# A two-layer spectral convolution kernel: the layout of small row loads in the last pass and of the spectrum tile in the second

## The reference, cut to what matters

```python
def _L0_conv_ref(x, weight_re, weight_im, bias):      # spectral convolution, 4 heads of 16 channels
    x_freq = jnp.fft.rfft2(x, axes=(-2, -1))
    core = jnp.einsum('bhixy,hioxy->bhoxy', xf[:, :, :, :32, :17], weight)   # 32 x 17 modes only
    out_freq = zeros.at[:, :, :, :32, :17].set(core)
    return jnp.fft.irfft2(out_freq, s=(H, W), axes=(-2, -1)) + bias

def _L1_conv_ref(x, gamma, beta):                     # a norm in hyperbolic space, over channels
    mu = m / sqrt(max(m[0]**2 - sum(m[1:]**2), EPS))  # m: mean of every channel over all pixels
    alpha = max(xf[:, 0] * mu[0] - xf[:, 1:] @ mu[1:], 1 + EPS)
    d = arccosh(alpha); var = mean(d * d)             # over all pixels of all images
    ...                                               # per pixel factors, then per channel
    return concatenate([sqrt(1 + sum(s * s)), s])

x = x + _L0_conv_ref(_gn(x), ...)
x = x + _L1_conv_ref(_gn(x), ...)
```

## Time and profile before

| what | us |
|---|---|
| median of three runs | 3980.3 |
| the three runs | 4032.01, 3980.3, 3980.14 |
| the profiled execution, its own time | 4024.94 |
| its span, first to last instruction | 4023.4 |
| first pass, roughly | 0 to 1120 |
| second pass | 1152 to 2060 |
| third pass | 2082 to 4023 |

### The profile page before, as it was taken

The page is one execution under the profiler, slowest core; times in us unless marked ns, Lnnn a source line. Parts: engine busy times, 40 slices in busy tenths (PEclk is TensorE's granted clock), DMA queues, the critical chain, the costliest instruction groups (busy, mean ns, idle before and its releaser), DMA issues. The chain is left out here.

```text
span 4023.4 us, 77883 instructions
## 1 busy us (share of the span) xinstructions
PE 3002.5 (75%) x26018; PEld 1495.1 (37%) x26018; DVE 2748.0 (68%) x2969; ACT 2141.8 (53%) x2940; POOL 1513.6 (38%) x876
## 2 busy tenths in 40 slices
PE   6988898989446767677715877877777778877776
PEld 3555555555211222222203434344333344443332
DVE  1888888888865355555444767677777677777766
ACT  6777676767200011111014767677776677776665
POOL 0110101010111111111113766666666666666666
PEclk9988888988668888888857999999999999999999
DMA  9878777677269999999915989899999899999898
GB/s 373 287 256 282 260 265 274 244 285 253 76 259 354 325 341 376 362 361 374 334 53 183 337 313 329 313 325 321 313 315 320 306 330 334 329 334 311 311 314 288
DMA packets 280512, 1199.08 MB, mean 298 GB/s; under 512 B 35145, under 2 KB 37038, under 8 KB 197934
## 3 DMA queue, kind: packets, MB, share of 16 engines
q1 hardware_dynamic: 266126, 1152.07, 79.9%
q0 software_dynamic: 14112, 43.37, 3.4%
HBM read 883.53 MB, written 311.73 MB: 297 GB/s over the span
## 5 line engine op out<-in xcount | busy, mean ns | idle before, releaser
L1323 POOL TENSOR_TENSOR c_ot<-c_ot,c_pp 128x1024 f32<-128x1024 f32 x512 | 1211.8, 2368 | 727.0 <-DVE c_ot L1272 651.8
L1262 DVE SCALAR_TENSOR_TENSOR c_xt<-c_xt,keep_k,c_p_u 128x1024 f32<-128x1024 f32 x512 | 654.0, 1277 | 332.5 <-DMA c_xt<-in_x 170.8
L1118 PE MATMUL c_p_u<-c_mv,c_zc 64*128 64x256 f32 x4096 | 612.3, 420 | 225.1 <-DVE c_xt L1262 163.1
L1272 DVE SCALAR_TENSOR_TENSOR c_ot<-c_p_f,keep_k,c_xt 128x1024 f32<-128x1024 f32 x512 | 657.3, 1284 | 177.0 <-DMA out<-c_ot 134.4
L1198 ACT ACTIVATE c_pp<-c_p_p,c_cols 128x1024 f32<-128x1024 f32 x512 | 570.5, 1114 | 362.4 <-PE c_p_p L1132 359.0
L1205 ACT ACTIVATE c_sq<-c_xt,c_cols 128x1024 f32<-128x1024 f32 x512 | 584.2, 1141 | 139.5 <-DVE c_xt L1262 138.8
L1118 PEld LDWEIGHTS c_p_u<-c_mv,c_zc 64*128 64x128 f32 x4096 | 371.4, 195 | 532.9 <-DVE c_xt L1262 321.3
L327 ACT ACTIVATE a_junk<-a_xt 128x1024 bf16<-128x1024 f32 x512 | 537.2, 1053 | 28.8 <-DMA a_xt<-in_x 21.5
L246 PE MATMUL a_p_rows<-a_xt,a_dft_h 128*64 128x512 f32 x2048 | 517.5, 652 | 33.6 <-DMA a_bias_t<-in_bias 19.5
L1132 PE MATMUL c_p_f<-c_rt,c_lwc 64*128 64x512 bf16 x1024 | 328.0, 402 | 179.6 <-DVE c_ot L1272 161.3
L663 PE MATMUL b_p_al<-b_xt,b_awc 128*32 128x512 f32 x2048 | 312.4, 682 | 161.2 <-DMA b_xt<-in_x 116.3
(11 more groups left out here) (209 smaller groups left out, 3029.8 us busy)
## 6 DMA issues: line engine op xcount, KB each, us to landing
a_xt<-in_x SPq DMA_DIRECT2D x256, 1024.0 KB, 8.0
b_xt<-in_x SPq DMA_DIRECT2D x128, 2048.0 KB, 16.0
c_xt<-in_x SPq DMA_DIRECT2D x256, 1024.0 KB, 16.7
out<-c_ot SPq DMA_DIRECT2D x256, 1024.0 KB, 18.4
maps<-b_maps POOLq DMA_DIRECT2D x64, 192.0 KB, 5.7
dmap<-b_dmap POOLq DMA_DIRECT2D x16, 768.0 KB, 11.6
c_rt<-maps SPq DMA_DIRECT2D x512, 24.0 KB
c_dmap<-dmap SPq DMA_DIRECT2D x16, 768.0 KB, 17.2
```

The lines of the kernel that those rows point to most:

```text
L1118: last = nc.tensor.matmul(p_u[:, 512 * at + W * r:512 * at + W * r + W], zc[t // CH][64 * at:64 * at + 64, i], mv[t % NB][64 * at:64 * at ...
L1262: V.scalar_tensor_tensor(out=u, in0=u, scalar=kc, in1=p_u[:], op0=ALU.mult, op1=ALU.add).then_inc(u_done, 1)
L1272: V.scalar_tensor_tensor(out=ot[t % NB][:, at], in0=p_f[:], scalar=kinv, in1=xt[t % NB][:, at], op0=ALU.add, op1=ALU.mult).then_inc(f_done, 1)
L1323: P.tensor_tensor(o, o, pp[n][:], ALU.add).then_inc(o_done, 1)
```

## The change

There are three edits.

1. **Third pass, rows of `rt`.** The rows are no longer the first 12 partitions of each half. They stand at partitions 5, 15, ... 115 (twelve rows, the two halves together), 14, 30, ... 126 (eight rows) and 16, 48, 80, 112 (four rows); `misc` masks follow. One load brings the rows of both halves, so a tile has three loads of 12, 8 and 4 rows in place of six of 6, 4, 2, 6, 4 and 2. The bytes are the same. The spectrum tile `ys` and its transform `idft` use every second partition of 128 in place of the first 64, and channel 0 goes out in one store in place of four.
2. **Second pass, spectrum tile.** `spt` and `prod` have 128 partitions with 32 channels each in place of 64 partitions with 64 channels. The sums over channels come out as two partial sums, on partitions 0 to 63 and 64 to 127, which the matmul of `layer_rows` adds, since `idft_h` now holds the transform twice. The factors by channel are copied once to `ah` and `lh` in the new layout. The modes come in four loads in place of two.
3. The semaphore counts follow.

```diff
+MAP_ROWS = ((5, 10), (14, 16), (16, 32))
...
-    for at, first in ((12, 0), (18, 64)):
-        for part, (row, rows) in enumerate(((0, 6), (6, 4), (10, 2))):
-            for s in range(2):
-                m[first + row + s:first + row + rows:2, at + 2 * part + s] = 1.0
+    for a, at in enumerate((12, 18)):
+        for part, ((first, step), rows) in enumerate(zip(MAP_ROWS, (6, 4, 2))):
+            for i in range(rows):
+                m[first + step * (rows * a + i), at + 2 * part + i % 2] = 1.0
...
-        spt = sb("spt", [64, C, YS])
-        prod = sb("prod", [64, C, M2])
+        spt = sb("spt", [128, C // 2, YS])
+        prod = sb("prod", [128, C // 2, M2])
...
-                for k in range(2):
-                    pool.dma_start(spt[KX * k:KX * k + KX].rearrange("k (h i) m -> k h (i m)", h=HEADS),
-                                   spec[b, k].rearrange("(h k) n -> k h n", h=HEADS)).then_inc(sp_in, 16)
+                for h in range(HEADS):
+                    half, i = 64 * (h // 2), 16 * (h % 2)
+                    pool.dma_start(spt[half:half + 64, i:i + 16].rearrange("p i m -> p (i m)"),
+                                   spec[b, :, KX * h:KX * h + KX]).then_inc(sp_in, 16)
...
-                ch.step(V.tensor_tensor(prod[:], spt[:, :, 0:M2], over_m(arow[0:64, b]), ALU.mult))
+                ch.step(V.tensor_tensor(prod[:], spt[:, :, 0:M2], over_m(ah[:, b]), ALU.mult))
...
-                V.tensor_reduce(vm[0:64, 0], prod[:].rearrange("p c m -> p m c"), AX_X, ALU.add).then_inc(v_ready, 1)
+                V.tensor_reduce(vm[:, 0], prod[:].rearrange("p c m -> p m c"), AX_X, ALU.add).then_inc(v_ready, 1)
...
+            for half in range(2):
+                p, c = slice(64 * half, 64 * half + 64), slice(32 * half, 32 * half + 32)
+                ch.inc(V.tensor_copy(ah[p], arow[p, :, c]))
+                ch.inc(V.tensor_copy(lh[p], lrow[p, :, c]))
...
-    maps_v = io["maps"].rearrange("b m s (t n) -> b t (m s) n", n=TC)
+    maps_v = io["maps"].rearrange("b (a m) s (t n) -> b t a (m s) n", a=2, n=TC)
...
+                for (first, step), rows in zip(MAP_ROWS, (6, 4, 2)):
+                    sp.dma_start(r[first:first + step * (2 * rows - 1) + 1:step], maps_v[b, t, :, :rows]).then_inc(r_in[t % NB], 16)
                 for at in range(2):
-                    for row, rows in ((0, 6), (6, 4), (10, 2)):
-                        sp.dma_start(r[64 * at + row:64 * at + row + rows], maps_v[b, t, 6 * at:6 * at + rows]).then_inc(r_in[t % NB], 16)
...
-                    sp.dma_start(ys[KX * k:KX * k + KX, 32 * half:32 * half + 32].rearrange("k (h i) m -> k h (i m)", h=2),
+                    sp.dma_start(ys[64 * k:64 * k + 64:2, 32 * half:32 * half + 32].rearrange("k (h i) m -> k h (i m)", h=2),
...
-                for j in range(4):
-                    sp.dma_start(o0_v[b, 0, j], o0[32 * j:32 * j + 32]).then_inc(o0_out, 16)
+                sp.dma_start(o0_v[b, 0], o0[:]).then_inc(o0_out, 16)
```

More of the change, by code:

```diff
@@ L578, in stage_b @@
     uw_ready, uw_out, aw_ready, var_ready = sem("uw_ready"), sem("uw_out"), sem("aw_ready"), sem("var_ready")
-    NC_IN = 16 * 16
+    NC_IN = 16 * 17
     with ExitStack() as mem:
@@ L595, in stage_b @@
         arow, lrow = sb("arow", [128, B, C]), sb("lrow", [128, B, C])
+        ah, lh = sb("ah", [128, B, C // 2]), sb("lh", [128, B, C // 2])
         aw, awc = sb("aw", [128, B, 2, 2]), sb("awc", [128, 2, 47])
@@ L634, in _ @@
             sp.dma_start(btrow[:], row(io["beta"], C)).then_inc(c_in, 16)
-            sp.dma_start(idft_h[0:64], cst["idft_d"]).then_inc(c_in, 16)
+            for half in range(2):
+                sp.dma_start(idft_h[64 * half:64 * half + 64], cst["idft_d"]).then_inc(c_in, 16)
             sp.dma_start(idft_w[:], cst["idft_w"]).then_inc(c_in, 16)
@@ L814, in combine @@
             def combine(b):
-                dve.wait_ge(sp_in, b * 32 + 32)
-                over_m = lambda a: a.unsqueeze(2).to_broadcast((64, C, M2))
-                ch.step(V.tensor_tensor(prod[:], spt[:, :, 0:M2], over_m(arow[0:64, b]), ALU.mult))
+                dve.wait_ge(sp_in, b * 64 + 64)
+                over_m = lambda a: a.unsqueeze(2).to_broadcast((128, C // 2, M2))
+                ch.step(V.tensor_tensor(prod[:], spt[:, :, 0:M2], over_m(ah[:, b]), ALU.mult))
                 if not is_at(b, 0):
                     dve.wait_ge(z_mm, b)
-                V.tensor_reduce(vm[0:64, 0], prod[:].rearrange("p c m -> p m c"), AX_X, ALU.add).then_inc(v_ready, 1)
-                V.tensor_copy(vm[0:64, 1], spt[:, 0, 0:M2]).then_inc(v_ready, 1)
+                V.tensor_reduce(vm[:, 0], prod[:].rearrange("p c m -> p m c"), AX_X, ALU.add).then_inc(v_ready, 1)
+                V.tensor_copy(vm[0:64, 1], spt[0:64, 0, 0:M2]).then_inc(v_ready, 1)
                 dve.wait_ge(v_ready, b * 3 + 2)
-                ch.step(V.tensor_tensor(prod[:], spt[:, :, 0:M2], over_m(lrow[0:64, b]), ALU.mult))
-                V.tensor_reduce(vm[0:64, 2], prod[:].rearrange("p c m -> p m c"), AX_X, ALU.add).then_inc(v_ready, 1)
+                ch.step(V.tensor_tensor(prod[:], spt[:, :, 0:M2], over_m(lh[:, b]), ALU.mult))
+                V.tensor_reduce(vm[:, 2], prod[:].rearrange("p c m -> p m c"), AX_X, ALU.add).then_inc(v_ready, 1)
                 dve.wait_ge(v_ready, b * 3 + 3)
@@ L892, in _ @@
             ch.inc(V.memset(uw[:], 0.0))
[L893 to L894 removed]
+            V.memset(vm[:], 0.0).then_inc(setup, 1)
             dve.wait_ge(c_in, NC_IN)
@@ L1074, in entry @@
                             load_modes(b + 1, half)
-            sp.wait_ge(zeroed, 2 * NB + 2)
+            sp.wait_ge(zeroed, 2 * NB + 3)
             for half in range(2):
                 load_modes(0, half)
-            sp.dma_start(idft[0:64].rearrange("p a b c -> p (a b c)"), cst["idft_c"]).then_inc(c_in, 16)
+            sp.dma_start(idft[0:128:2].rearrange("p a b c -> p (a b c)"), cst["idft_c"]).then_inc(c_in, 16)
             sp.dma_start(misc[:], cst["misc"]).then_inc(c_in, 16)
@@ L1095, in _ @@
             store_channel_0(B - 1)
-            sp.wait_ge(o0_out, B * 64)
+            sp.wait_ge(o0_out, B * 16)
         @block.tensor
@@ L1164, in _ @@
             pe.wait_ge(c_in, 16 * (2 + 2 * NB))
-            pe.wait_ge(filled, 3)
+            pe.wait_ge(filled, 2)
             for part in range(8):
@@ L1239, in _ @@
             columns(0)
-            act.wait_ge(zeroed, 2 * NB + 2)
-            act.wait_ge(filled, 3)
+            act.wait_ge(zeroed, 2 * NB + 3)
+            act.wait_ge(filled, 2)
             for part in range(8):
@@ L1298, in _ @@
             V.memset(ys[:], 0.0).then_inc(zeroed, 1)
-            V.memset(idft[64:128], 0.0).then_inc(filled, 1)
+            V.memset(idft[:], 0.0).then_inc(zeroed, 1)
             V.memset(p_z[:], 0.0).then_inc(filled, 1)
```

4 lines of the change are left out of this document (2 added, 2 removed).

## The result

The changed kernel takes 4329.3 us (median of four runs, 4317.8 to 4342.7), the one before 3994.8 (median of four, 3980.1 to 4032.0). The ratio is 1.082, with a 95% interval of 1.073 to 1.091: slower by 8%, about 330 us, where 108 were forecast. The time lies above the range. The profiled execution has a span of 4330.6 us.

What follows compares the result with a forecast made beforehand. DMA, paced by two leading engines, bounds the third pass; the modes' chain and the DMA limit alternate in the second. Third pass 75, second 33 and once 3 sum to 111 us, 108 against the 3980 median: 4088 us, range 3930 to 4160.

Steps and rivals of the forecast that it cites:

- The landing of the modes: Second pass: each load of 64 rows on two engines, eight in all with 75.8 kB; modes land 7 us later an image.
- `combine`, -6.5 us an image: Second pass, VectorE: multiplications and reductions on half the elements a partition take 7.2 us in place of 13.7.
- landing unchanged: Second pass, far bound: modes land no later and the pass runs at 376 in place of 356 GB/s, -46 us.
- The issues, +1.7 us: Second pass: four issues of modes loads in place of two, 0.56 us each or up to 0.88, +1.7 us an image.
- The dealing by a number that divides both sides: Small loads: rows go in equal shares to engines whose number divides both sides; +4.1 kB a tile on two leading engines.
- The rival that GpSimd's queue shares evenly: Second pass: GpSimd's queue deals by destination, modes load on 16 engines, -40 us there; total 4015 us, chance 0.14.
- An issue blocks when one engine's queue is full: SP's loads of 37 rows: each issue held up 6.7 us, 148 kB at one engine's rate of 22 GB/s.
- The third pass, +75: Third pass: 7.2 kB more on leading engines, 0.31 us a tile, 75 us over 245 tiles; lower bound +20 us.
- SP's three saved issues give nothing: Third pass: three fewer SP issues a tile, 0.29 us each, lie beside its blocking and gain nothing.
- the spacing changes nothing: Third pass: spreading `rt`, `ys` and `idft` over partitions changes neither row counts nor a matmul's shape, so no time.
- The rival by partitions written to: Third pass: rows are dealt by destination partitions, -129 us; total 3805 us, or 3884 with modes on few engines; chance 0.14.
- The cap of 376 GB/s: Second pass: the first pass's rate, 23.5 GB/s for each of 16 engines, taken as the DMA limit.

## Why the prediction was wrong, point by point

**The landing of the modes: the step that failed.** The prediction put 75.8 kB on eight engines in all, two a load, and said "Bounds for 37.9 kB more: 1.6 us, its bytes at 23 GB/s, and 12 us"; it took 7. The wait grew by 24.8 us an image. The engines were right: two a load and eight in all is what the starts of the packets show. What failed is that the term counted bytes only, and gave the engines without data nothing to do. An entry of GpSimd's queue takes its turn with packets of `x`, which take 0.70 us each (16.4 kB at 23.5 GB/s; 0.66 to 0.74 in the records of the waits). 64 turns are 45 us, where the entries of modes ran from 7.5 to 46.9 us after the first issue in the image shown first, and from 4.0 to 48.5 in the first of the pass; 8 turns before are 5.6. Every engine had the 64, also those without any data, and in nine of 16 images only these were waited for. Of the 348 us that the unequal loads cost the second pass, rows of 4 KB take away 242; the run with equal sides shows that the shape of the loads is the whole of it, the one with the old tile that nothing else of the edit is needed.

**`combine`, -6.5 us an image: right.** 7.2 us was forecast and measured. With equal loads, which give the edit without the landing, the kernel gained 47 us, and the prediction's bound for "landing unchanged" was 46. The gain was there, and the longer wait, 24.8 us an image, took nearly four times the 6.5.

**The issues, +1.7 us: right.** 4 x 0.682 for 2 x 0.562 is +1.6.

**The dealing by a number that divides both sides: right.** The prediction had it from one load, that of 37 rows. It gives 2 for 64 rows against two blocks, and the packets show that: 128 of data, 896 empty ones, and starts that about eight engines would give for four loads. The rival that GpSimd's queue shares evenly fell with them; the -40 us it gave the second pass came only where the sides were made equal, as -47.

On SP's queue the records tell it too. There a transfer has one packet of 4 bytes, its end, for each engine that carried its data, and in the third pass these are all the packets under 512 B. First before, then the third pass's edit alone, in 2500 to 3700 us:

```profile
DMA packets 64704, 386.19 MB, mean 322 GB/s; under 512 B 11455, under 2 KB 11455, under 8 KB 22060
```

```profile
DMA packets 61875, 381.42 MB, mean 318 GB/s; under 512 B 9371, under 2 KB 9371, under 8 KB 19739
```

| in 2500 to 3700 us | ends | loads of `x` | ends a tile | by common divisors | 8 and 4 rows on 8 and 4 engines |
|---|---|---|---|---|---|
| kernel before | 11455 | 165 | 69.4 | 69 | |
| third pass's edit | 9371 | 164 | 57.1 | 57.25 | 65.25 |
| the same, four stores | 9975 | 164 | 60.8 | 61 | 69 |
| three loads of 12 rows | 14388 | 178 | 80.8 | 81 | |

The 69 are 32 of `x` and `ot`, 6 + 4 + 2 + 2 twice for the rows of `maps` and `bmap`, and 9 for a sixteenth of an image's nine other transfers; the 57.25 have 12 + 2 + 2 + 2 + 2 for the rows and 4 ends of the single store in place of 64. So loads of 6, 4 and 2 rows ran on 6, 4 and 2 engines, those of 8 and 4 rows against two blocks on two each, and the single store on four. The loads of 37 rows have one end each (5 ends among 745 packets in the 34 us of the earlier trace rows), and the sixteen of 32 and 5 rows 168, which is 8 x (16 + 5).

**"An issue blocks when one engine's queue is full": borne out.** At the end of SP's second to eighth issue of 37 rows, 260 to 269 of the packets of 1 KB issued so far had not started, each time; and the load of `x` behind them, which uses all 16 engines, was held up for 6.50 us while fifteen stood idle. With 32 + 5 rows it isn't held: the two issues of `x` take 0.83 us together.

**The third pass, +75: right sign, too large.** Two leading engines do set its pace: three rows fewer on each gave 6.75 us a tile as worked out. Each load of `x` and each store of `ot` lands in 16 parts. In the kernel before, 2500 to 3700 us, the 15th part comes 4.9 us after the 14th and the last 7.6 us, in the median of 332 transfers, where the first 14 lie within 2.9 us. With the pass's edit alone it is 8.3 and 9.1 us, in the changed kernel 8.8 and 9.4, and with three loads of 12 rows 0.3 and 1.5. Which two of the 16 they are the records don't say. SP's long issues of these rows go the same way: over 1.5 us are 35 of 1536 before, 46 of 768 in the changed kernel and 3 of 768 with three loads of 12 rows. But alone the edit cost 30 us, near the lower bound of 20. By the medians the rows cost 15 us where 43 were put for them, the store 15 where 32 were. The prediction named a reason and gave it no size: "If the small transfers cost these engines something beyond their bytes, three fewer give back a part." At 0.03 to 0.04 us each that would be 22 to 29 us over 245 tiles, the size of what is missing in the rows. But that price is as uncertain as its run, and the run with three loads of 12 rows, which has three transfers fewer too, came out at 6.75 us a tile by its bytes alone. Why the pass lost less than forecast isn't settled.

**"SP's three saved issues give nothing", "the spacing changes nothing": wrong, and they cancelled.** The spaced loads cost SP 0.562 us in the median, 1.69 for three (the one with 12 rows takes some 0.8, so rather 1.9 a tile), and the six before 6 x 0.287 = 1.72. With six spaced ones the kernel lost 173 us.

```profile
L1038 SPq DMA_DIRECT2D c_rt<-maps x768: 499/562/5877, 2432.4 to 4292.4; - x192
```

**The rival by partitions written to: fell.** The third pass's edit with four stores has the rows spread over the partitions, and its three loads cost SP only some 1.9 of 7.33 us a tile; the rival had that pass 129 us faster, and the kernel took 15 us more than before. (The run with six spaced loads doesn't bear on it, since SP bounds it.) No run here shows the spread to help these small loads.

**The cap of 376 GB/s** isn't one: it is what the first pass moved in the earlier trace rows, and the second with equal loads and rows of 16 KB; the first pass of the changed kernel moved 385 in the same stretch. With 4 KB rows the second pass moves 389. The wait for modes went from 393.3 to 301.4 us with them, 92 us, and the kernel's time by 88, so shorter turns could be all of that gain; whether short rows move faster by themselves wasn't tried.

**The sum.** 75 + 33 + 3 = 111 us became 108 on the way to the median, where the share of 1.1% would have made it 110. It changes nothing.

What would have shown it beforehand: the earlier trace rows have landings up to 32.6 us for only 38 kB an engine. Bytes can't give that; turns behind 16 KB rows can, those of the modes and those of the loads and stores ahead of them in GpSimd's queue (in the image with the latest landing the first packet of modes started 17.1 us after the first issue). The prediction used that row's minimum and left its maximum alone.

## What to carry to other kernels

Write both sides of a small DMA with the same outermost count, 32 and 32 here, even where a view with fewer and longer blocks looks neater: 64 rows against two blocks made the second pass 348 us longer, and 37 rows in place of 32 + 5 the kernel 37. Afterwards compare the packet count of its queue with the bytes it moves (28960 for 14112 packets here, at the same 43 MB). Beside the stream of `x` a load of GpSimd cost as many turns as it put entries on one engine, empty ones too (64 an image for 8), each about as long as one row of the stream (0.70 us with 16 KB), so few entries and short rows of the stream mattered more here than bytes. And where small loads ran on the same few engines, these set the pace of the pass (two of 16 landed 4.9 and 7.6 us after the rest; 6.75 us a tile for 7.25 once they had three rows fewer): count their kilobytes, and the issuing engine's time for each load too (0.54 us for spaced rows, 0.29 for adjacent ones).

## What the runs showed that was not expected

- A load dealt to two engines still puts packets on the other 14: 14336 of 8 bytes more in the queue of GpSimd, and the load isn't done until they are. In nine of 16 images VectorE waited 22 to 29 us for them after the last byte had come.
- Rows of 4 KB in place of 16 KB raise the rate of the second pass from 359 to 389 GB/s in 1152 to 1900 us, and the whole kernel gains 88 us; with equal loads on the new tile they give the pass only 30.
- Issuing a load with spaced partitions costs SP 0.54 to 0.56 us in the median (0.75 with 12 rows each), for 0.29 with adjacent ones.
- A pass bound by DMA became faster with half more bytes of `maps`, 6.75 us a tile for 7.25 before.
